# Attention into mixture of experts on one core: the last unit's weighing is put ahead of the first gate and up products, and its maxima rows are spread by ScalarE alone

## The reference, cut to what matters

```
scores = einsum('bhsd,bhtd->bhst', qh, kh) / sqrt(8);  scores = where(mask == 0, -1e9, scores)
out = einsum('bhst,bhtd->bhsd', softmax(scores), vh) @ wO.T + bO          # 16 heads of 8
expert = argmax(LN(x) @ router.T)
y = (silu(xe @ gate[e].T) * (xe @ up[e].T)) @ down[e].T                   # 352 wide
```

## Time and profile before

| | |
|---|---|
| runs | 289.07, 293.77, 294.06 us |
| median | 293.77 us |
| the profiled execution | 290.8 us, of which its span is 288.7 us |
| mean granted TensorE clock | 0.954 |
| TensorE busy | 243.0 us, 84% of the span |
| ScalarE busy | 163.3 us, 57% |
| VectorE busy | 186.7 us, 65% |

### The profile page before, as it was taken

The page is one execution under the profiler, slowest core; times in us unless marked ns, Lnnn a source line. Parts: engine busy times, 40 slices in busy tenths (PEclk is TensorE's granted clock), DMA queues, the critical chain, the costliest instruction groups (busy, mean ns, idle before and its releaser), DMA issues.

```text
span 288.7 us, 5570 instructions
## 1 busy us (share of the span) xinstructions
PE 243.0 (84%) x1842; PEld 135.6 (47%) x1858; DVE 186.7 (65%) x659; ACT 163.3 (57%) x304; POOL 105.2 (36%) x124
## 2 busy tenths in 40 slices
PE   0799999698498999999999899999878798569991
PEld 0335756456354455554545454545442354245550
DVE  3191875947979968878898888696822257324440
ACT  1167474424126797778789878878873231333440
POOL 2542683621701611114311413131366124565533
PEclk9999999959889999999999999999995799998998
DMA  6990355332183779830006999500089221766400
GB/s 179 408 422 39 103 137 148 91 100 73 50 183 97 168 222 309 209 91 2 3 0 172 410 368 321 150 30 17 0 303 325 97 79 49 223 225 210 149 18 10
DMA packets 20811, 44.67 MB, mean 155 GB/s; under 512 B 1670, under 2 KB 15757, under 8 KB 19824
## 3 DMA queue, kind: packets, MB, share of 16 engines
q1 hardware_dynamic: 9296, 30.63, 33.1%
q10 hardware_dynamic: 9824, 10.00, 12.0%
q0 software_dynamic: 1664, 3.69, 3.7%
HBM read 30.90 MB, written 13.93 MB: 155 GB/s over the span
## 4 chain that ended last, share of the span: by engine, by line
PE 39%; ACT 11%; issue 7%; DVE 7%; another core or an unknown queue 2%; POOL 2%; POOLq 0%; DVEq 0%
PE banks L1348 9%; ACT p_region L742 7%; PE banks L1418 7%; PE banks L1333 6%; PE banks L1262 5%; PE banks L1445 3%; DVE scores_unused L1013 3%; ACT banks L750 3%; PE banks L1127 1%; PE banks L1434 1%; PE banks L1329 1%; PE banks L1425 1%; PE banks L1133 1%; POOL binned_dram L590 1%
## 5 line engine op out<-in xcount | busy, mean ns | idle before, releaser
L1013 DVE CUSTOM_DVE_ANT_0 scores_unused<-banks,mask_bias 128x512 bf16<-128x512 f32 x128 | 83.1, 687 | 12.1 <-PE banks L1262 11.3
L742 ACT ACTIVATE p_region<-banks 128x1024 f32<-128x1024 f32 x64 | 63.8, 1020 | 21.2 <-PE banks L1333 20.9
L1262 PE MATMUL banks<-k_region,q_region 80*128 80x512 bf16 x128 | 48.1, 388 | 3.4 <-DVE max L1013 3.2
L1333 PE MATMUL banks<-q_region,k_region 80*128 80x256 bf16 x256 | 45.9, 272 | 4.9 <-ACT banks L750 2.8
L572 POOL COPY q_region<-q_region 8x768 bf16<-8x768 bf16 x16 | 13.0, 814 | 65.1 <-ACT q_region L726 65.0
L1333 PEld LDWEIGHTS banks<-q_region,k_region 80*128 80x128 bf16 x256 | 24.3, 98 | 26.0 <-issue 5.2
L496 POOL TENSOR_TENSOR ln_rstd<-ln_var_eps,minus_half 128x2 f32<-128x2 f32 x16 | 12.2, 764 | 61.5 <-DVE ln_var_eps L821 61.5
L750 ACT ACTIVATE banks<-mask_bias_by_key 128x1024 f32<-128x1024 bf16 x31 | 31.9, 1030 | 1.0
L1348 PE MATMUL banks<-p_region,values 128*9 128x256 f32 x512 | 32.2, 394 | 0.0
L1418 PE MATMUL banks<-k_region,q_region 128*64 x64 | 24.8, 514 | 3.2 <-issue 2.3
L778 ACT ACTIVATE q_region<-banks 128x352 f32<-128x352 f32 x16 | 7.4, 465 | 33.3 <-PE banks L1419 24.2
(11 more groups left out here) (148 smaller groups left out, 453.9 us busy)
## 6 DMA issues: line engine op xcount, KB each, us to landing
binned_dram<-ctx_region ACTq DMA_DIRECT2D x2, 4626.0 KB, 24.4
k_region<-experts_dram SPq DMA_DIRECT2D x17, 544.0 KB, 3.7
k_region<-k_parts_dram SPq DMA_DIRECT2D x4, 1152.0 KB
k_region<-experts_dram SPq DMA_DIRECT2D x1, 3808.0 KB, 19.2
q_region<-q_parts_dram SPq DMA_DIRECT2D x12, 192.0 KB
k_region<-mask1k_dram SPq DMA_DIRECT2D x1, 2048.0 KB, 11.7
k_region<-mask_dram SPq DMA_DIRECT2D x1, 2048.0 KB, 16.0
k_parts_dram<-q_region SPq DMA_DIRECT2D x4, 384.0 KB, 2.8
```

Of the source, the lines that this page charges most:

```text
L742: a.activation(pt[:, u % 2, j, :, :].rearrange("p (c t) q -> p c (t q)", c=2), ps[:, c:c + 2, :], ACT.Exp, scale=float(D1) ** -0.5).then_i ...
L1013: return v.tensor_tensor_reduce(out=junk[:, q, :], in0=scores, in1=m1b[:, QT * (u // 4) + q, :], scale=1.0, scalar=-3e38, op0=ALU.add, op1 ...
L1262: return m.matmul(out, qst[0:R, (u * GH + j) * SQ + q * P:(u * GH + j) * SQ + (q + 1) * P], kst[0:R, (u * GH + j) * SK:(u * GH + j + 1) * ...
L1333: last = m.matmul(out[:, t * SQ:(t + 1) * SQ], kst[0:R, k:k + P], qst[0:R, (u * GH + j) * SQ:(u * GH + j + 1) * SQ], start=False, stop=Tru ...
```

## The change

On TensorE `weigh(15)` stands between `step(-2)` and `step(-1)`; `turn_out(15)` stays behind `step(-1)`. On ScalarE `copy_out(15)` moves in the same way ahead of `step(-1)`. For unit 15 alone ScalarE copies the eight rows of maxima to all four heads in one instruction, the source broadcast, and both GpSimd's copy and TensorE's wait for `rows_set` fall away.

```
 # GpSimd
             inverse_root("s4", 2)
-            rows_of_maxima(15)
             for s in range(ROWS_SOONER // 2):
                 rows_in(s)
 # ScalarE, minus_max_rows(u)
+                heads = 1 if u + 1 < UNITS else GH
-                emptied(a.activation(qst[0:MROWS, u * GH * SQ:(u * GH + 1) * SQ], src, ACT.Copy), f"X{u}")
+                dst = qst[0:MROWS, u * GH * SQ:(u * GH + heads) * SQ].rearrange("p (j q) -> p j q", j=heads)
+                emptied(a.activation(dst, src.unsqueeze(1).broadcast_to([MROWS, heads, SQ]), ACT.Copy), f"X{u}")
 # ScalarE, end
-            pipeline(step, -2, 0)
+            pipeline(step, -2, -1)
             copy_out(UNITS - 1)
-            pipeline(step, 0)
+            pipeline(step, -1)
 # TensorE, scores_k
-                if j == 1 and c == 0:
+                if j == 1 and c == 0 and u + 1 < UNITS:
                     pe.wait_ge(rows_set, u + 1)
 # TensorE, end
-            pipeline(step, -2, 0)
+            pipeline(step, -2, -1)
             weigh(UNITS - 1, 0)
             weigh(UNITS - 1, 1)
+            pipeline(step, -1, 0)
             turn_out(UNITS - 1)
             pipeline(step, 0)
```

## The result

The changed kernel takes 291.90 us (median of 20 runs, 290.09 to 295.40) and the kernel before, measured beside it, 290.68 us (20 runs): a ratio of 1.0087, 95% interval 1.0059 to 1.0115. This ratio compares only the runs within 1.5% of their kernel's quickest, which leaves out nine of the 20 runs of the kernel before and two of the changed one (and, in the two experiments run last, 14 of 17 of the kernel before, because one at 273.63 us lies alone); over all 20 and 20 the ratio of the means is 1.0037, interval 1.0000 to 1.0076. So the change costs 0.4 to 0.9% where it should have gained 1%: forecast were 290.0 us from a level of 292.8, that is a ratio of 0.990. The time lies in the range, and so near to 290.0 only because that level was 2.1 us too high. The profiled execution of the changed kernel is the quickest of its 20, 290.09 us with a span of 287.3, against 290.8 and 288.7 before.

What follows compares the result with a forecast made beforehand. TensorE was taken as the bound from 218 to 225, then held 1.7 us by a PSUM copy. 1.8 (or 0.8) plus 1.4 (or 0) minus 0 (or 0.66), taken as 2.8: 292.8 - 2.8 = 290.0 us, range 286.4 to 294.8.

Steps and rivals of the forecast that it cites:

- level of 292.8: Starting time for the subtraction, halfway between the four executions' mean 291.9 and the three runs' median 293.77.
- The edit to the maxima's rows: ScalarE's copy for unit 15 grows from 8x256 to 8x1024, 0.66 us more; costed at 0, other end 0.66.
- Case 4: Slower: late last exponential leaves TensorE empty, clock returns one stretch of work later; 1.6 us lost, 294.4, chance 0.13.
- The hole: ScalarE idle 1.65 us until 215.82, read as waiting for program behind three expert loads; its end should stay at 215.8.
- the second case: ScalarE's longer copy not swallowed by its idle stretch: last exponential 218.7, gain 2.1, 290.7 us, chance 0.13.
- The order: Unit 15's weighing and copy before step 0's gate and up: TensorE's 1.7 us idle before the turning vanishes or halves.
- 1.8 or 0.8: Gain in us at step 1's gate and up, starting at 225.3 or 226.3 instead of 227.07.
- 1.06 us without a row: Unit 15's weighing: 4.54 us until ScalarE's copy started, against 3.48 by its own records; difference unexplained.
- case 3: Unit 15's copy waited for program behind four loads, and tanh or another copy then waits; gain 0 to 1.0, chance 0.22.
- The clock: TensorE busy without a hole from 218.2 until beyond 229, so the second clock fall (227.95) disappears: 1.4 us, or 0.
- GpSimd's part: GpSimd loses its 0.81 us copy, first four gathers come some 0.9 us earlier, a wait is dropped: 0.
- the three signs of a wrong forecast: Clock falling again at 228; ScalarE hole between weighing and tanh; gain at 228 gone by 260 in a longer hole.

Runs made afterwards that it cites:

- the two experiments run last: On the quick chip: changed kernel with five unread products added and GpSimd's later gathers delayed, 281.21 us; kernel before with only the new order, 278.20 us.
- the idle time filled: Changed kernel plus five unread 128x512 TensorE products before unit 13's turning, against the kernel before: 0.9942 on the quick chip, 0.9961 on another.
- The slower kernel: Changed kernel plus an unread 8x768 GpSimd copy that brings its gathers back to their old time, against the kernel before on the quick chip: 1.0056.
- the four loads are moved: Changed kernel with the four expert loads started only when unit 15 is turned, against the kernel before: 1.0091.
- the order alone: Kernel before with unit 15's weighing and copy moved ahead, maxima's rows as before: 1.0005 and 0.9966; third time, on the quick chip, 278.20 us.
- the gathers held: Changed kernel with GpSimd's batch 2 scatter and second four gathers waiting until unit 15 is turned, against the kernel before: 1.0004.

## Why the prediction was wrong, point by point

**The edit to the maxima's rows** is the step that failed, in both directions in which it argued. Its size was right: ScalarE's copy grew by 0.64 us (1.00 against 0.36), forecast 0.66. "0.66 of 1.65 us disappear in it. I cost it at 0" was wrong: the last exponential is later by 0.55 to 0.89 us in five traces of kernels with the edit on the three chips, and by 0.56 on the quick chip with the clock whole. In the changed kernel there was no hole left to swallow anything; the copy of unit 14 (L734, 213.98) was let go by its own product. On the three chips these 0.55 to 0.89 us are a sum of several things: the longer copy, the slow weighing, and against them the hole that went. With the idle time filled the last exponential there is at +9.69, some 0.5 us ahead of the 10.16 to 10.29 without the edit. And the upper bound was no bound, since the price is not paid on ScalarE alone. "Queued behind it are the copy of the router's transposed rows" stood in the text, but who waits for that copy was never asked. It is TensorE, whose idle time went from 0.62 to 1.26 us, and behind it the clock was at 0.50 for 3.4 us. The edit was costed at nothing because only ScalarE's own line was followed. Filling the idle time takes 1.49 us off the path on the quick chip (15.39 to 13.90), and the copy itself is the remaining 0.57 (13.90 against 13.33). In whole times that is 280.93 against 277.63 us there, more than the 1.49 of the place. The slower kernel has a second low stretch, 243.8 to 247.2 behind an idle time of 1.96 us, and the filled one has none although it idles 2.13 us in the same place; by the end of the two spans the distance is 2.2 us. The slower kernel also has the copy added on GpSimd, and that was not run apart; the changed kernel itself was never run on the quick chip. Case 4 named a clock that comes back later behind a late exponential, but at 217.5, not at 209, and was given 0.13.

**The hole** was misread. It was taken for the engines' next piece of program behind three loads. The late signal of a product explains it better: unit 14's weighing ended at 213.85 in the kernel before, and was seen at 215.80, while the gathers had been issued until 214.96. No program packet ended any of these holes, and they move with the gathers, fail to appear on one chip, and stay when the four loads are moved. The page of the Trainium skill (Runtime: NRT & Kernel Launch, Instruction fetch mechanics), by which such a fetch is mostly hidden, was therefore not contradicted by this hole: the trace of before was no evidence against it, and the second case built on it, that the 0.66 is paid, was the true one for that term on the quick chip (0.57); its reason, a hole that moves with ScalarE's order, was not.

**The order.** What it removes was named rightly. The quick chip shows it: step 1 starts 0.80 us earlier (14.13 to 13.33), which was the lower end of the term "1.8 or 0.8", and TensorE's wait ahead of the turning is gone. The output is earlier by the same 0.80. The upper end counted 1.06 us without a row as time to be won. It was the late signal, and on the chip of the profile it was not removed but met twice, at the copy (2.16 us after its product) and at the tanh (3.67). On the three chips step 1 still starts 0.57 to 0.65 us earlier with the order alone, but the output is 0.16 to 0.24 later. That is case 3 as to what happens (the copy waited for something else, and then the tanh waits too) with the wrong something: gathers, not loads. Its price, gain 0 to 1.0, can be neither confirmed nor refused for the order alone (1.0005 and 0.9966, all 1.0037 and 1.0008).

**The clock.** "From 218.2 TensorE now has work without a hole" failed with it. Instead TensorE has 1.08 and 2.69 us of idle time between 220.6 and 224.8, and the second low stretch begins at 223.0 and lasts 6.8 us where it had begun at 228.0 and lasted 3.4. From step 1 to the output it took 4.50 us before and 5.28 in the changed kernel, 5.31 with the order alone: instead of the 1.4 us forecast as gain, 0.8 are lost here, more than the order alone had gained. The first of the two old low stretches (217.7) did go, as the weighing at 217.08 took 1.91 us and not 3.48; it was exchanged for the one at 209.3.

**GpSimd's part** was put at 0. On the quick chip nothing speaks against it. On the three others the traces do: without the edit to the maxima's rows GpSimd issues its fourth gather until 7.2 us behind the start of exponential 58 and unit 14's copy is 1.9 us late, with it (and these gathers not moved otherwise) the issue ends at 6.1 and the copy starts at most 0.45 us behind its product. The earlier gathers most likely gave back part of what the longer copy cost; that was not run apart there.

**What the profile was to show:** the weighing from about 218.2 (217.08), L734 ahead of L779 (yes), turning directly behind the transpose (no, 1.08 us), one low stretch (no), unit 14's copy still at 215.8 (no, 213.98), output product ended 228.3 to 228.7 (229.95). Of the three signs of a wrong forecast, two came: a clock that falls again, though at 223 and not at 228, and a hole on ScalarE between the weighing and the tanh.

**Sums in it.** 3.2 less half of the 1.06 us is 2.7 and not 2.8, a last exponential 0.66 later would move 218.35 to 219.0 and not 218.85, and 294.4 with a microsecond of scatter is 295.4 and not 294.8. None of these decides anything here; the level of 292.8 against a measured 290.68 does, since it hides a miss of 3.9 to 4.0 us in the gain (2.8 forecast, a loss of 1.1 to 1.2 us measured as the difference of the two means and the two medians) behind a time that is 1.9 us off.

**A better version.** The changed kernel with the five filling products is faster than the changed kernel on the one of the three chips where it ran (0.9935), and on the quick chip faster than the changed kernel with GpSimd's copy added (0.9885, interval 0.9858 to 0.9913). Against the kernel before it is 0.6% faster on the quick chip; on the other the gain, 0.4% or over all runs 0.2%, cannot be told from none. On the quick chip it does no better than the order alone (277.63 against 278.20 us), so there the maxima's rows need not be touched.

## What to carry to other kernels

When an instruction on one engine grows by half a microsecond, follow each small copy that is queued behind it to the engine that waits for it, and ask what that engine's idle time will be; a wait of TensorE that grows by 0.64 us can cost more through its clock than by itself (1.49 us here). A hole that the trace puts on nobody is not time to be won and not cover either until a run has moved it; here it moved when another engine's issuing of transfers was moved. And a gain on a chain that is released by such late signals shows only on a chip that doesn't have them, so compare distances within the trace before the totals.

## What the runs showed of the hardware that was not expected

- Signals of TensorE's finished products were seen 1.1 to 4.9 us late, where an engine waited for them, while GpSimd issued a row of indirect transfers (about 0.95 us each), by the semaphores' own times in the trace, and several of them then came within 0.1 us. Where the row of gathers ended behind unit 15's weighing, the last late copy or tanh started 1.15 to 1.33 us after the last gather's issue had ended, in eleven traces out of eleven. Signals early in such a row were on time (0.02 us), and with the gathers held one came before the row's end, so issuing alone is not the condition. This was so on three chips and in none of the six traces of the fourth, on which the kernel before takes 279.4 us instead of 291.0 to 291.9. How the issuing and the signals are joined is open; no run took the gathers' work away without moving it.
- No packet of the instruction queues moved during the two holes of the changed kernel (216 to 224 us), though the trace puts them on "another core or an unknown queue".
- TensorE's clock was at 0.50 for 3.4 us right behind idle times of 1.26 us in one piece or 1.28 us in three, in ten traces out of ten, and whole when it idled 0.62 or 0.18 us in the same place. The idle time alone does not decide it: elsewhere the clock stayed whole behind 1.84 us (changed kernel, 258.5) and behind 2.13 us (filled, 242.1).
- A ScalarE copy out of PSUM of 8 partitions takes 1.00 us for 1024 elements each and 0.36 for 256. A copy of 128 partitions with 256 elements takes 0.36 as well, and one with 1024 (the bias) 1.03: the price goes by the length, and eight partitions cost as much as 128.
